# First cross attention: the norm's mix and the next group's values change places, the squares move behind the scores

## The reference

```python
q = x @ Wq.T + bq; k = ctx @ Wk.T + bk; v = ctx @ Wv.T + bv      # 16 heads of 8, ctx: 77 rows a sequence
# a small network (w1, b1, w2, b2, w3, b3) takes three features of each sequence and head,
# among them a mean and a variance over the scores and the weights, to a temperature
# weights = softmax(scores / temperature); out = (weights @ v) @ Wo.T + bo
x = _layernorm(x + out)
```

## Time and profile before

| | |
|---|---|
| median of 3 runs | 1966.23 us (1959.42 to 1967.46) |
| the profiled execution: time, span | 1969.08 us, 1967.4 us |
| mean granted clock of TensorE in it | 0.916 |
| busy over the whole span | PE 1662.6 (85%), DVE 1277.6 (65%), ACT 1203.5 (61%), POOL 471.6 (24%) |
| busy from 736.00 to 1026.30, this stage | PE 222.50, DVE 215.97, ACT 206.06, POOL 173.81 of 290.30 us |

### The profile page before, as it was taken

One profiled execution on the slowest core, in us unless ns is written; L12 is line 12 of the kernel. 1 busy time (PEld: TensorE's weight loads), 2 busy tenths in 40 slices (PEclk: granted clock), 3 DMA queues, 4 the chain that ended last, 5 costly groups with the idle time before them and its releaser, 6 DMA issues. The chain is left out here.

```text
span 1967.4 us, 28934 instructions
## 1 busy us (share of the span) xinstructions
PE 1662.6 (85%) x10514; PEld 950.8 (48%) x10514; DVE 1277.6 (65%) x1731; ACT 1203.5 (61%) x2567; POOL 471.6 (24%) x396
## 2 busy tenths in 40 slices
PE   3999999999999735888776856999999999589976
PEld 1444444444343312666554523666666666356655
DVE  0778777777777629888717442666566666388854
ACT  2777787778777613878852343565555556267764
POOL 0111011111111105767610000222222223145540
PEclk9999999999999956899985687999999999689987
DMA  4000000000000000000000010000000000000001
GB/s 123 1 11 1 0 6 6 0 0 0 0 0 1 0 18 7 8 5 2 2 4 0 1 43 1 1 1 1 1 1 1 1 1 1 17 9 9 2 3 48
DMA packets 36804, 16.77 MB, mean 9 GB/s; under 512 B 15334, under 2 KB 35520, under 8 KB 36672
## 3 DMA queue, kind: packets, MB, share of 16 engines
q1 hardware_dynamic: 32512, 9.11, 2.1%
q10 hardware_dynamic: 4160, 5.90, 0.9%
HBM read 12.90 MB, written 2.10 MB: 8 GB/s over the span
## 5 line engine op out<-in xcount | busy, mean ns | idle before, releaser
L1998 POOL TENSOR_TENSOR self_probs<-self_probs,self_rz 128x1024 f32<-128x1024 f32 x64 | 121.3, 1895 | 535.6 <-DVE self_rz L2026 535.6
L525 POOL TENSOR_SCALAR gru_decay<-gru_zgate 128x512 f32<-128x512 f32 x96 | 75.5, 786 | 591.0 <-ACT gru_zgate L478 565.6
L1973 ACT ACTIVATE self_probs<-self_scores,self_neg 128x128 f32<-128x128 f32 x512 | 181.4, 385 | 16.7 <-DVE self_neg L2021 16.7
L389 PE MATMUL gru_gate<-gru_xn,gru_whg 128*128 128x512 f32 x384 | 182.2, 597 | 3.5 <-DVE gru_xn L568 3.5
L393 PE MATMUL gru_hid<-gru_xn,gru_whg 128*128 128x512 f32 x384 | 180.5, 592 | 0.0
L401 PE MATMUL gru_out<-gru_y,gru_wo 128*128 128x512 f32 x384 | 178.1, 599 | 0.7 <-DVE gru_y L596 0.7
L1137 ACT ACTIVATE x_pt<-x_turned 77x512 f32<-77x512 f32 x256 | 137.4, 585 | 63.5 <-PE x_turned L1035 62.3
L1035 PE MATMUL x_turned<-const_ident,x_probs 128*77 128x128 f32 x1024 | 143.8, 285 | 23.4 <-POOL x_probs L1186 12.3
L1035 PEld LDWEIGHTS x_turned<-const_ident,x_probs 128*77 128x77 f32 x1024 | 116.2, 151 | 75.5 <-POOL x_probs L1186 26.9
L591 DVE SCALAR_TENSOR_TENSOR gru_ghid<-gru_hid,gru_half_c,gru_sighid 128x512 f32<-128x512 f32 x96 | 71.8, 748 | 113.4 <-ACT gru_sighid L479 113.3
L596 DVE TENSOR_TENSOR_SCAN gru_y<-gru_decay,gru_value 128x516 f32<-128x516 f32 x96 | 118.3, 1232 | 3.3
(11 more groups left out here) (359 smaller groups left out, 3566.9 us busy)
## 6 DMA issues: line engine op xcount, KB each, us to landing
gru_whg<-in_L_attn_Whg ACTq DMA_DIRECT2D x4, 768.0 KB, 10.4
x_ctx_in<-in_ctx SPq DMA_DIRECT2D x16, 154.0 KB
gru_xin<-in_x SPq DMA_DIRECT2D x8, 256.0 KB, 2.9
out<-moe_y SPq DMA_DIRECT2D x8, 256.0 KB, 2.3
gru_wo<-in_L_attn_Wo ACTq DMA_DIRECT2D x4, 384.0 KB, 11.3
self_w_raw<-in_L_attn_Wq SPq DMA_DIRECT2D x1, 512.0 KB, 6.1
self_w_raw<-in_L_attn_Wk ACTq DMA_DIRECT2D x1, 512.0 KB, 6.9
self_w_raw<-in_L_attn_Wv SPq DMA_DIRECT2D x1, 512.0 KB, 9.3
```

What stands on the lines that cost most here:

```text
L389: mm(ps_gate[n % 2][:, :], whg[:, l, k, DI + c * P:DI + (c + 1) * P], xn[u][:, k, :], start=(k == 0), stop=(k == KH - 1))
L1973: last = f(probs[n % 2][:, a, jj, :], ps_s[n % 2][:, a, jj * T:(jj + 1) * T], ACT.Exp, bias=neg[n % 2][:, a, jj:jj + 1], accum_out=z[n % 2 ...
L1998: pool.tensor_tensor(probs[n % 2][:, :, :, :], probs[n % 2][:, :, :, :], whole, ALU.mult).then_inc(pn_ready.sem, 1)
```

## The change

In PLACES (with temper, the first cross attention alone), the second place of slot 2 and the first place of slot 3 are exchanged: mix and y move from slot 3 to the end of slot 2, values and their copy from there into slot 3. The square of y moves from behind turn 3 to the head of slot 3, behind the scores.

```diff
@@ -853,7 +853,7 @@
         if temper:
-            PLACES = [(("context", 1), ("keys", 1)), (("queries", 1), ("t1", -1)), (("t23", -1), ("values", 1)), (("mix", -3), ("var", -3))]
+            PLACES = [(("context", 1), ("keys", 1)), (("queries", 1), ("t1", -1)), (("t23", -1), ("mix", -3)), (("values", 1), ("var", -3))]
         else:
@@ -882,12 +882,12 @@
             ORDER += [("scores", n, 0), ("kbd", n + 1, 0), ("pre", n - LE, 0)]
+            ORDER += [("square", g - 3, 0)] * (r == 3)
             ORDER += [("turn", n - LT, 0), ("turn", n - LT, 1), ("logs", n - LA - 1, 0), ("scale", n - LA - 1, 0)]
             ORDER += [("divide", g - 4, 0)] * (r == 0)
             ORDER += place(n, 0, False) + place(n, 0, True)
             ORDER += [("soft", n, 0), ("sums", n - 1, 0)]
             ORDER += [("turn", n - LT, 2), ("turn", n - LT, 3)]
-            ORDER += [("square", g - 3, 0)] * (r == 3)
             ORDER += [("exp", n - LE, 0), ("attend", n - LA, 0)]
```

## The result

| | before | after |
|---|---|---|
| median of 8 runs each | 1966.87 us (1959.42 to 1970.37) | 1973.17 us (1968.61 to 1977.74) |
| span of the profiled execution | 1967.4 us | 1972.6 us |
| mean granted clock of TensorE | 0.916 | 0.912 |

The changed kernel takes 1.0036 of the time, interval [1.0023, 1.0049]: 6 to 7 us more. The forecast was +0.65 us and a time of 1966.9; the measured one lies above the range, which ended at 1971.

The account below looks back on a forecast made before the run. DVE was taken to bound the loaded part, ACT and PE the drain. Terms -2.1, -1.3, +0.84, +1.44 and +1.77 sum to +0.65 us, so a median of 1966.9; range 1960 to 1971, the forecast's own 1963 to 1970.

Parts of the forecast that it names:

- Loaded slots 3, -0.52 each: Sequences 15, 19, 23, 27: var no longer waits for the square, next scores and maximum 0.52 us earlier; -2.1 in all.
- Costs put at nothing: Loaded slots: y's wait for the mix, square holding pt, the shared bank's order, earlier scores; all taken as 0.
- Slots 10 and 11, -1.3: No mix there: DVE's wait for the values goes in slot 10, their copy returns in slot 11; -1.3 us net.
- Slot 31, +0.84: Last loaded slot: mix and y in slot 30 push the maximum, oT and attend later; var +0.84 us.
- Slots 35 and 39, +1.44 and +1.77: Drained slots: the square waits for y and holds pt on ACT, delaying the chain behind by 1.44 and 1.77 us.
- The sum: The edit-by-edit addition of all terms, in times of the profiled execution: +0.65 us.
- rival C: Clock turns against the change: more low parts in loaded groups; four more groups give +7.6, 1974.5 us; chance 0.07.
- Rival A: The drain costs nothing, the held pt being caught up at the next wait; 1962.8 us; chance 0.18.
- Rival B: Var in loaded slots 3 waits for the values' copy or shared bank instead; -2.1 falls away, 1969.0 us; chance 0.10.
- Rival D: Clock turns for the change: the three low parts in loaded slots go; -4.25, 1962.0 us; chance 0.07.

Follow-up runs that it names:

- h1: Changed kernel plus products nobody reads (12, 4 and 4) on PE in front of attend in slots 31, 35 and 39; 1971.87 us, ratio 1.0033.
- h2: As h1, with 5 more such products in front of turn 2 in slots 32, 35, 36 and 39; 1975.34 us, ratio 1.0041 to the kernel before.
- cut pairs: Kernel before and changed kernel, both ended behind the first cross attention (means 1029.7 and 1033.0 us) or behind the first feed-forward (1170.4 and 1173.4).
- The one left out above: Trace of the changed kernel ended behind the first cross attention, from an execution over 1.5% above its fastest, left out of the means; 1044.01 us.

## Why the prediction was wrong

Lengths in all traces that bear on it, from DVE's rows: first maximum to the maximum of sequence 28 (loaded), and from there to the last divide (drain), with the time at the low clock up to the last but one divide (twice the missing share of the mean clock). "Tail" is the order of slots 28 and later, "loaded" that of the slots before. The kernel with slot 31 alone counts as old loaded; it, the swap alone and h1 and h2 are in no row of the tail.

| order | loaded | drain | low in it |
|---|---|---|---|
| old tail, 8 traces | | 82.2 (81.4 in five, 81.6, 82.3, 86.4) | 3.2 |
| new tail, 7 traces | | 88.3 (85.8 to 92.8) | 8.8 |
| old loaded, 9 traces | 200.1 | | |
| new loaded, 7 traces | 196.7 | | |

The differences and their standard errors are +6.1 and 1.2 for the drain, +5.6 and 3.1 for the low clock in it, -3.4 and 0.9 for the loaded part.

- *Loaded slots 3, -0.52 each:* right in mechanism. It is 30.03 - 29.58 = 0.45. The copy of the values costs the same in its new place, but y at the seam costs 0.97 to the next start (897.09 to 898.06) and not 0.89. DVE's queue releases the bank behind y in both orders, so why the next instruction starts 0.07 later here is not shown.
- *Costs put at nothing:* the square ahead of pt, the bank's order, y's wait for the mix (0.51) and the scores came out so. They cost nothing in the loaded part.
- *Slots 10 and 11, -1.3:* from maximum 10 to maximum 12 the changed kernel takes 14.10, at full clock; the kernel before takes 17.2 to 17.4 with a low part there and 14.94 without. So -0.84 like with like, within the bounds. But against the trace that the prediction was made from, 17.40, it is -3.3: six of nine traces of the old loaded order have a low part there, none of ten of the new. The low parts fall elsewhere instead, 57.1 us in the loaded part before and 56.6 after. The gains together were predicted as -3.4 and are -3.4 in the mean of the traces, which is partly luck: like with like the rows give four times 0.45 and 0.84, 2.6.
- *Slot 31, +0.84:* right at full clock. In the second trace of the changed kernel, which has next to no low clock up to the last but one divide (0.7 us, right at the start), it is 22.40 + 7.81 against 20.83 + 8.46 from the maximum of 28 to the next divide, +0.92.
- *Slots 35 and 39, +1.44 and +1.77:* +1.97 and +1.71 between the divides in that trace (25.26 for 23.29, 22.28 for 20.57). The drain as a whole: 85.82 against 81.37, +4.45 for a predicted +4.05. So the mechanism of these terms was right, and their size nearly so.
- *What failed:* the step from the rows to "The sum", which priced slot 31 and the drain at the clock of the profiled execution, +4.05, and so put the low clock in the drain at nothing. It came in as rival C alone, in the loaded groups ("if four more groups went down") and with a chance of 0.07. It is in the drain that it came: 8.8 us of low clock in the mean instead of 3.2. With the +4.45 it makes a mean difference of +6.1, so 1.7 are the clock's (with a standard error of 1.2, this part is not clear of noise). Less the 3.4 of gains the stage is at +2.7, which agrees with +3.2 and +3.0 of the cut pairs. On the whole kernel +6.5 was measured. That is 5.9 above the forecast; of these the stage's traces account for 2.0 and the cut pairs for 2.4 to 3.8, and the rest stays open.
- *Rival A (the drain costs nothing):* refuted by the kernel with the new tail alone, and by the drains, 85.8 or more in each trace of the new tail. *Rival B (var is not freed):* refuted by the rows above. *Rival D (three low parts go):* did not come; the low clock in the loaded part stayed the same.
- *The range* also carried an error of method: it stood on a profiled execution of 1969.08 and a median over three runs, while the same kernel spreads over 1958.6 to 1976.4 in 35 runs, and it ended 4 us above the forecast.

Open: why the low clock is more frequent in the new drain. Of nine traces with the new slot 31 and no fillers, seven have a fall of the clock 2.7 to 4.8 us behind the slot's maximum; of eight with the old one none has (one has a long low part that runs through it). The one left out above has it too. That is an association: the two traces with fillers lack this fall, so do two without, and what brings it about is not shown.

## What to carry to other kernels

When a step is moved inside a software pipeline, walk the fill and the drain as carefully as the steady state: here the same edit gained 0.45 us in each of four loaded groups and lost 4.45 in slot 31 and the drain at full clock, where the step has nothing to stand in for. An order list can be given the new order for the loaded groups and the old one for the rest; that kernel lost nothing that could be measured. Where two traces put their difference into a stage whose code is the same, compare the granted clock there and take more traces, or kernels cut short behind each stage, before explaining it.

## What the runs showed of the hardware

- One stage of fixed code, the feed-forward, took 132.0 to 143.1 us in 13 traces, the longer the lower its mean granted clock (0.71 down to 0.63). What decides that clock is not shown; the instant of its first rise does not (22.2 us behind the start with 132.0, 22.6 with 142.55).
- 36 executions with 0.93, 2.40 or 3.39 us more on the path were too few to show in the time what that costs: the interval of a ratio over 12 is 7 to 9 us wide.
- In the changed kernel's drain the clock fell 1.5 us behind the end of a wait of PE of 2.07 us; in another trace of the same kernel the same wait was followed by over 50 us at full clock.
- A float32 product of 128x128 by 128x128 took 0.24 us at full clock in a row of twelve, in two records each (2.84 us, x24).
- Behind y, where DVE's queue waits for y's own end and then releases the bank (L1286), DVE stood 0.21 us before its next instruction.
